# Later DMA issues, four load buffers, and the projection weights cast last, in an attention and FP4 kernel

## The reference, cut to what matters

```
xn = layernorm(x)
s  = attn(xn):      # 16 heads of 64
     q, k, v = rmsnorm(xn) @ qkv_w.T ;  q, k = exp(-0.5 q*q), exp(-0.5 k*k)
     kv  = k.T @ v  (per head, over all 2048 rows of a sequence)
     out = (q @ kv) / (q . sum(k) + 1e-6)
     x2  = xn + gamma * (out @ proj_w.T + proj_b)
     s   = x2 + gamma * (gelu(rmsnorm(x2) @ conv1_w.T + conv1_b) @ conv2_w.T + conv2_b)
g  = silu(ffn(xn)): # every operand of its matmuls quantised in blocks of 16 to FP4 values
     h = silu(Q(xn) @ Q(w_gate).T) * (Q(xn) @ Q(w_up).T) ;  ffn = Q(h) @ Q(w_down).T
out = x + s * g
Q(x): scale = max|block of 16| / 6, values rounded to 0, 0.5, 1, 1.5, 2, 3, 4, 6 times scale
```

## Time and profile before

| | |
|---|---|
| three runs, us | 1999.74, 2073.59, 1997.06 (median 1999.74) |
| profiled execution, us | 1997.77 |
| its span (slowest core, core 1), us | 1996.2; the other cores 1979.4 to 1993.6 |
| mean granted TensorE clock by core | 0.977 to 0.980 |
| busy share of the span | TensorE 94%, VectorE 82%, ScalarE 39%, GpSimd 20% |

### The profile page before, as it was taken

The page is one execution under the profiler, slowest core; times in us unless marked ns, Lnnn a source line. Parts: engine busy times, 40 slices in busy tenths (PEclk is TensorE's granted clock), DMA queues, the critical chain, the costliest instruction groups (busy, mean ns, idle before and its releaser), DMA issues.

```text
span 1996.2 us, 27757 instructions; the slowest of 8 cores (1979.4 to 1996.2 us)
## 1 busy us (share of the span) xinstructions
PE 1875.5 (94%) x9142; PEld 879.4 (44%) x9142; DVE 1636.2 (82%) x2019; ACT 785.3 (39%) x991; POOL 395.5 (20%) x356
## 2 busy tenths in 40 slices
PE   6988697878999999999999999999999999999997
PEld 3434343333444444444444444444444444444443
DVE  4788878867688688797734999999999999999986
ACT  4676576664433433544521222222222222222221
POOL 3245545534423422422500000000000000000000
PEclk9999898989999999999999999999999999999998
DMA  9788778884455465465599433444334333433322
GB/s 301 199 238 233 226 210 212 229 225 127 115 159 161 109 174 161 101 189 149 127 197 191 126 103 88 95 102 103 94 86 105 103 93 86 105 99 92 88 83 66
DMA packets 367262, 287.07 MB, mean 144 GB/s; under 512 B 299024, under 2 KB 308240, under 8 KB 366096
## 3 DMA queue, kind: packets, MB, share of 16 engines
q1 hardware_dynamic: 367120, 285.29, 55.3%
HBM read 153.63 MB, written 59.24 MB: 107 GB/s over the span
## 4 chain that ended last, share of the span: by engine, by line
PE 71%; DVE 8%; issue 7%; DMA 6%; ACT 3%; POOL 3%; SPq 2%; DVEq 0%; ACTq 0%; POOLq 0%
PE PS L1081 30%; PE PS L1126 15%; PE PS L900 10%; PE PS L883 8%; PE PS L840 5%; DMA xf<-w_gate 2%; DMA wst<-c1T 2%; PE PS L646 1%; DVE q_am L222 1%; DVE atz L817 1%; DVE ob L256 1%; PE PS L588 1%; DVE xf L231 1%; DMA xf<-w_up 1%; DMA phi_h<-pq 1%
## 5 line engine op out<-in xcount | busy, mean ns | idle before, releaser
L240 ACT ACTIVATE gam<-xf 128x1024 bf16<-128x1024 f32 (+1 forms) x196 | 198.1, 1011 | 505.1 <-DVE xf L231 494.5
L1081 PE MATMUL PS<-wg,xqT 128*128 128x512 bf16 (+1 forms) x1536 | 319.9, 361 | 1.7 <-DVE so L910 1.7
L1081 PE MATMUL PS<-wu,xqT 128*128 128x512 bf16 (+1 forms) x1536 | 319.9, 361 | 0.0
L222 DVE TENSOR_REDUCE q_am<-xf 128x64 f32<-128x1024 f32 (+1 forms) x196 | 227.6, 1161 | 74.5 <-DMA xf<-w_up 29.5
L250 DVE SCALAR_TENSOR_TENSOR xf<-gam,xf 128x1024 f32<-128x1024 bf16 (+1 forms) x196 | 233.9, 1193 | 30.0 <-ACT gam L240 29.7
L256 DVE SCALAR_TENSOR_TENSOR ob<-gam,q_sc 128x1024 bf16<-128x1024 bf16 (+1 forms) x196 | 243.0, 1240 | 3.3 <-DVE gam L253 2.8
L231 DVE SCALAR_TENSOR_TENSOR xf<-xf,q_rc 128x1024 f32<-128x1024 f32 (+1 forms) x196 | 238.0, 1214 | 1.9
L253 DVE SCALAR_TENSOR_TENSOR gam<-gam,xf 128x1024 bf16<-128x1024 bf16 (+1 forms) x196 | 235.6, 1202 | 2.1
L883 PE MATMUL PS<-xn2T,c1T_s 128*128 128x512 bf16 x1024 | 234.8, 384 | 2.4 <-DVE kvbd L566 2.4
L1126 PE MATMUL PS<-wdA,hqT 128*128 128x512 bf16 x1024 | 227.8, 380 | 0.4 <-DMA hqT<-ob 0.4
L900 PE MATMUL PS<-c2T_s,hdd 128*128 128x512 bf16 x1024 | 222.3, 379 | 0.0
(11 more groups left out here) (90 smaller groups left out, 1852.8 us busy)
## 6 DMA issues: line engine op xcount, KB each, us to landing
xx<-x SPq DMA_DIRECT2D x32, 512.0 KB, 4.5
xf<-x SPq DMA_DIRECT2D x32, 512.0 KB, 4.2
xr<-x SPq DMA_DIRECT2D x32, 512.0 KB, 4.6
out<-xr SPq DMA_DIRECT2D x31, 512.0 KB, 3.9
xa<-x SPq DMA_DIRECT2D x30, 512.0 KB, 6.0
stg<-qkvT SPq DMA_DIRECT2D x24, 512.0 KB, 13.2
xf<-w_gate SPq DMA_DIRECT2D x22, 512.0 KB, 6.3
xf<-w_up SPq DMA_DIRECT2D x22, 512.0 KB, 5.9
```

The costliest lines, as they stand in the source:

```text
L222: S.add("v", lambda v: v.tensor_reduce(am, blk(y), AX, op.max, apply_absolute_value=True), waits=[src_ev, opt("q_nq%d" % (k - 3))], ev="q_ ...
L240: S.add("sc", lambda s: s.activation(gam[k % 2][:, 0:W], xf[k % 3][:, 0:W], AF.Abs, scale=BIG), waits=["q_y%d" % k, opt("q_out%d" % (k - 2 ...
L1081: S.add("pe", lambda pe, wts=wts, bi=bi, j=j, b0=b0, ic=ic: pe.matmul(bank(b0 + j, GB[bi][1]), xqT[t % 3][:, ic, :], wts[bi][:, ic, :], st ...
```

## The change

- **Issues by SyncE.** The store of a quantised task, the store of q's result, the transpose of `turn` and the load of a tile of x are no longer emitted on SyncE's list where their data is made, but later: the first after the first step of the next period (`send`), the others at the start of the next group of matmuls (`held`).
- **Task buffers.** Tasks 0 to 27 use four buffers; the fourth lies in the place of `projT`. Their loads are emitted two tasks ahead instead of one. From task 28 on there are three buffers and one task ahead.
- **Weight jobs.** The order is now `2`, `1`, `2`, `1`, ... for 32 jobs and then the eight `p`. Jobs 0 to 19 use four buffers and their loads are emitted four ahead, after group 2; the others two, after group 1. The `p` casts wait for task 27 to leave the fourth task buffer.
- **Sequence change.** `zero_acc(1)` moves from the end of tile 16 to the end of tile 17.
- **Tail.** `turn(31)` moves from tile 27 into the tail, the loads of `phq`, `gb` move later there, that of `c2b` earlier. The last eight q groups have seven buffers instead of three.
- **Attention.** From tile 4 on its result lies in four banks with two blocks each, so `attn_z` makes one `den` and one `atz` instruction instead of three and three. `conv1` uses banks 4 to 7, the `y` pairs are (0, 1) and (2, 3). The second normalisation (`xn2`) is emitted later than the rest of `proj`, as `proj_xn2`.

```
+        xf4 = at("xf3", [P, D], F32, W1 + 12288)
+        wst = [... for i, o in enumerate([WK + 65600, WK + 69696, W3 + 24576, W3 + 28672])]
+        pqx = [at("pqx%d" % i, [P, 512], BF16, WK + 24576 + 1024 * i) for i in range(4)]
+        KX = 28
+        def xslot(k): return k % 4 if k < KX else k % 3
+        def xbuf(k): return xf4 if xslot(k) == 3 else xf[xslot(k)]
+        def xfree(k):
+            had = [j for j in range(max(k - 4, 0), k) if xslot(j) == xslot(k)]
+            return opt("q_nq%d" % had[-1]) if had else None
...
                 if n == 1:
+                    send()
                     mid()
...
+            def post(k):
+                unsent.append(lambda: store(k))
...
-                if i + 1 < len(tasks):
-                    load_task(tasks[i + 1])
+                while nload < len(tasks) and nload <= (i + 2 if nload < KX else i + 1):
+                    load_task(tasks[nload])
+                    nload += 1
...
-            S.add("sy", lambda s: s.dma_start_transpose(out=xn1T[:, c, :, :], in_=xn1_of(t)[:]),
+            later.append(lambda: S.add(
+                "sy", lambda s: s.dma_start_transpose(out=xn1T[:, c, :, :], in_=xn1_of(t)[:]),
...
+        for i in range(16):
+            wjobs += [("2", i, 0), ("1", i // 2, i % 2)]
+        wjobs += [("p", ic, 0) for ic in range(8)]
+        NW4 = 20
+        def wbuf(n): return n % 4 if n < NW4 else n % 2
...
+                w = ["wc%d" % (NW4 - 1), "wc%d" % (NW4 - 2)] if kind == "2" and ic >= 12 else \
+                    ["q_nq%d" % (KX - 1)] if kind == "p" else []
...
+        def held():
+            for fn in [later.pop(0) for _ in range(len(later))]:
+                fn()
...
         def q_group(s, qc):
+            held()
...
+            if n >= 56:
+                i = (n - 56) % 7
+                pb, sem = (pqx + [pq[2], pq[0], pq[1]])[i], "PX%d" % i
...
-                if gi == 1 and t > 4:
-                    while nl < min(nw + 2, len(wjobs)):
+                if gi == (2 if nl < NW4 else 1) and t > 4:
+                    while nl < min(nw + (4 if nl < NW4 else 2), len(wjobs)):
                         load_w(nl)
                         nl += 1
...
+            if t == 17:
+                zero_acc(1)
+            if t > 4:
+                kv_mm(t - 1)
             if t == 16:
-                kv_mm(t - 1)
                 evac(0)
-                zero_acc(1)
...
-        XB = [3, 4, 5, 2]
-        YB = [(0, 1), (6, 7)]
+        XB = [4, 5, 6, 7]
+        YB = [(0, 1), (2, 3)]
...
+            if s:
+                views = [(0, 4, 4, PS[:, 0:2048].rearrange("p (a x) -> p a x", a=4)[
+                    :, :, 0:260].rearrange("p a (h c) -> p a h c", c=65))]
...
-                          "atz3", "kvbd1_5", bfree[3], bfree[4]]
+                          "atz3", "x2_3", bfree[4]]
...
             kv_group(28 + n // 2, 2 + n % 2)
+            if n < 4:
+                proj_xn2(n)
+                turn_xn2(n)
...
+                if nxt and oc in (10, 12, 14):
+                    proj_xn2(4 * (s + 1) + (oc - 10) // 2)
```

More of the change, by code:

```diff
@@ L313, in xn_task, with send, store @@
                 tk["ev"] = "q_xn%d" % k
+        unsent = []
+        def send():
+            while unsent:
+                unsent.pop(0)()
         def stored(tk):
-            def post(k):
+            def store(k):
                 S.add("sy", lambda s: s.dma_start(out=tk["dst"], in_=ob[k % 2][:, 0:tk["W"]]),
@@ L512, in load_w @@
                 return
+            b = wbuf(n)
+            before = [m for m in range(n) if wbuf(m) == b]
             kind, ic, h = wjobs[n]
             src = {"p": "projT", "1": "c1T", "2": "c2T"}[kind]
-            S.add("sy", lambda s: s.dma_start(out=wst[n % 2][:],
+            S.add("sy", lambda s: s.dma_start(out=wst[b][:],
                                               in_=g[src][ic, :, D * h:D * (h + 1)]),
-                  waits=[opt("wc%d" % (n - 2))], inc="WS%d" % (n % 2), ev="wl%d" % n)
+                  waits=["wc%d" % before[-1] if before else "kvm3"], inc="WS%d" % b,
+                  ev="wl%d" % n)
         def cast_w(n):
             kind, ic, h = wjobs[n]
+            b = wbuf(n)
             if kind == "1":
-                S.add("sc", lambda s: s.activation(c1T[:, ic, D * h:D * (h + 1)], wst[n % 2][:],
+                S.add("sc", lambda s: s.activation(c1T[:, ic, D * h:D * (h + 1)], wst[b][:],
                                                    AF.Identity, scale=s2_fm[:, ic:ic + 1]),
@@ new lines, in attn_z @@
+            for h0, na, nh, v4 in views:
+                S.add("v", lambda v, h0=h0, na=na, nh=nh, v4=v4: v.tensor_scalar(
+                    den[b][:, h0:h0 + na * nh].rearrange("p (a h) -> p a h ()", a=na),
+                    v4[:, :, :, 64:65], 1e-6, None, op.add),
+                    waits=["at%d" % t, opt("zz%d" % (t - 2))], ev="den%d" % t)
+            S.add("v", lambda v: v.reciprocal(zz[b][:], den[b][:]),
+                  waits=["den%d" % t, opt("atz%d" % (t - 2))], ev="zz%d" % t)
@@ new lines, in attn_z @@
+            for h0, na, nh, v4 in views:
+                S.add("v", lambda v, h0=h0, na=na, nh=nh, v4=v4: v.tensor_tensor(
+                    atz[b][:, 64 * h0:64 * (h0 + na * nh)].rearrange(
+                        "p (a h e) -> p a h e", a=na, e=64),
+                    v4[:, :, :, 0:64],
+                    zz[b][:, h0:h0 + na * nh].rearrange("p (a h) -> p a h ()", a=na)
+                    .broadcast_to([P, na, nh, 64]), op.mult),
+                    waits=["zz%d" % t, opt("atT%d" % (t - 2))] +
+                          ["ps%d" % n for n in (56, 57, 58, 59, 63)], ev="atz%d" % t)
@@ L923, in build @@
             q_group(s, qc)
-            if n == 4:
+            if n == 1:
+                turn(31)
+                S.add("sy", lambda y: y.dma_start(
+                    out=c2b_t[:], in_=g["c2b"].rearrange("d -> () d").broadcast_to([P, D])),
+                    waits=["wc38"], inc="GC", ev="c2b_l")
+            if n == 8:
                 load_phq(0)
-            if n == 5:
+            if n == 10:
                 S.add("sy", lambda y: y.dma_start(
@@ L929, in build @@
                     waits=["xn1T31", "xn1T30"], inc="GB", ev="gb_l")
-                S.add("sy", lambda y: y.dma_start(
-                    out=c2b_t[:], in_=g["c2b"].rearrange("d -> () d").broadcast_to([P, D])),
-                    waits=["wc38"], inc="GC", ev="c2b_l")
                 S.add("gp", lambda p: p.tensor_tensor(gb[:], gb[:], gm[:], op.mult),
```

127 lines of the change are left out of this document (67 added, 60 removed).

## The result

The changed kernel took 1953.91 us (median of four, 1950.48 to 1954.67) against 1999.74 before. Compared on one chip the ratio is 0.9774, interval 0.975 to 0.9798: 45 us, or 2.3%. The forecast was 1948. Ratios and means of cores leave out executions and dies that ran a long stretch at a lower clock than the rest; where too few were left, no ratio is given.

A forecast was written before the change was run, and what follows sets the result against it. TensorE was busiest, its waits in the first 430 us mostly due to SyncE's order, with VectorE the limit after 209 us. Terms 12 + 38 - 7 + 5 + 2 = 50 us off 1997.8 gave 1948 us, range 1922 to 1985.

The forecast's parts named there:

- loads and issues: First 430 us: 59 of ScalarE's 96 us of waits go with more buffers and later issues, gaining 38 us.
- the zeroing: Sequence change: TensorE's 9.3 us wait for VectorE's copies goes, at 1.3 per idle us, gaining 12 us.
- covered: Deferred task stores: only ob's next writer waits, two tasks (14 us) later, so no cost was counted.
- projection casts last: Tiles 23 to 27: eight GpSimd casts instead of five slow VectorE, costing 7 us.
- 430 to 560 us: ScalarE's 5.2 us wait before the copies of v goes, less 2 us for tail loads: gain 5 us.
- attention: Attention over 28 tiles: one `atz` instead of three saves 0.28 us of VectorE each, gaining 2 us.
- the scaled task: ScalarE's waits for VectorE's scaled task: half, 16 of 31.9 us, go because its load comes earlier.
- Floor: 60 to 430 us: larger of VectorE's and TensorE's work sums to 308 of 370 us; at most 62 winnable.
- Half of it (1975): Rival: VectorE limits after the extra buffers end, so only the first stretch and zeroing gain; 1975 us, chance 0.27.
- GpSimd in tiles 23 to 27: Rival: extra casts delay the statistics there and take 15 of the 50 us; 1963 us, chance 0.12.
- Slower, by loads ahead of the transposes: Rival: earlier weight loads delay xn1T transposes in the DMA queue, 66 us lost; 2014 us, chance 0.06.
- All of it (1929): Rival: every wait on a load goes and only the floor is left, 69 us in all; 1929 us, chance 0.08.

The follow-up runs named there:

- u_zero: Changed kernel with zero_acc(1) put back to the end of tile 16; ratio to the kernel before 0.9777.
- p_zero: Kernel before with only zero_acc(1) moved to the end of tile 17; ratio to the kernel before 0.9982.
- u_now: Changed kernel with q's stores, transposes and loads of x issued at once again, task stores still late; ratio to the kernel before 0.973.
- u_order: Changed kernel with the old mixed order of weight jobs and three task buffers throughout; ratio to the kernel before 0.9832.
- u_kx: Changed kernel with three task buffers and one task ahead for all tasks; ratio to the kernel before 0.9808.

## Why the prediction was right or wrong

**Near in the total, wrong in the steps.** The sum was 50; the ratios give 45, the milestones 41.5. That is luck in part: up to tile 28 the forecast was 15 us too high, for the attention stage 9 too low. The step that failed most is that of loads and issues, 38 us forecast and about 17 measured; the next are the zeroing (12 forecast, 1 measured), which priced a stall of TensorE in a stretch that VectorE limits, and the store that was "covered" (0 forecast, 6.4 measured).

| step | forecast | measured |
|---|---|---|
| zeroing later | +12 | +1 undone (u_zero), +1 to +7 alone (p_zero) |
| loads and issues | +38 | task buffers 11, weight buffers 4 to 6, stores 1, issue order 0: about 17 |
| projection casts last | -7 | 0 to +2.6 |
| 430 to 560 us | +5 | +2.7 by milestone, +1 to +2 undone up to `conv1` |
| attention | +2 | +10.8: stores 6.4, `atz` 4.6 |

**Zeroing.** What failed was the 9.3 us wait that "goes", times 1.3, counted to the end. The wait went and 12.0 us with it (p_zero), but the same text had found VectorE the limit from 209 us on, in the very stretch. A TensorE stall in a stretch that VectorE limits is mostly made up; the two statements were not put side by side.

**Loads and issues.** Two parts of the step held: weights (40.3 to 10.1, forecast 8) and VectorE's own loads (56 to 6.6). "I take half, 16 of 31.9" for the scaled task failed: it rose to 39.6, and where a row shows it, at 236.93 us, VectorE's own work makes it late. q's stores (9.2 to 13.0) went up too. So of ScalarE's 96 us 23 went, not 59. The rest of the step, that the later issues free SyncE and with it the loads, failed in u_now: they give nothing, and SyncE stands as long behind q's results with them as without. The buffers did the work. "Statistics: `turn(31)` is emitted two groups later and more" was counted as a gain of 4 us of waits; in its place TensorE stands 9.0 us for tile 31's transpose. If the parts simply add, which nothing shows, and each has an error of some 3 us, 4.6 of the 30.1 us at `conv1` (30.1 less 11.3, 5.3, 1.6, 3.1, 1.1 and 3.1) belong to parts not undone: q's seven buffers and the moves in the tail.

**Floor.** By the prediction's own rule, the larger of VectorE's and TensorE's work in each stretch, the floor after is 130 + 95 + 82 = 307 us; 308 was forecast, and the stretches took 339.5. The size was right, though "gets no less work" hid that VectorE would lose 10 us more beside casts. Half of the 62 us above the floor was won. The floor should have cut the likeliest value, not only the high end.

**Projection casts.** The loss of VectorE was near: 4.0 us by u_order and u_kx, 6.5 forecast. "I charge all of it" failed, since the stage did not grow by it. What the new order gives back, around tile 25, u_order shows; by which wait is not settled. The 3.3 us for a cast had its own wait of 1.0 in it, so a cast can take 2.35 us from VectorE, and not 3.3.

**Attention.** Two failures. That the deferred store "is covered" looked at who waits for the store and not at what SyncE could do meanwhile; 142 us of standing there was in the trace of before, and the prediction read SyncE's waits in the first stage alone. And 1.3 for an idle microsecond was carried over from the first stage; in the attention stage the low clock behind five waits of 2.2 to 2.6 us cost another 1.6 each.

**The rivals.** Half of it (1975): by tile 23 19.3 us had come where it has 22.5; then, against it, 8 more up to tile 28 and 11 in the attention stage. GpSimd in tiles 23 to 27: its wait (`mrs`) fell from 14.9 to 10.8. Slower, by loads ahead of the transposes: apart from that of tile 31 TensorE waited once for a transpose, 2.7 us, 4.5 before, at a DMA share of up to 0.96. All of it (1929): the stretches stayed 32 us above the floor. Of the signs named, TensorE's idling (34, not under 30) and the stage's end (28 us sooner, not 35 to 50) were missed; that on weights was missed by a hair (10.1, not under 10); those on task loads, the 9.3 us and VectorE's share (89%) came true. One sign of being wrong came true as well: with tile 31 the waits for `xn1T` are 11.7 us, over 10. Its cause is not the one that the rival names.

## What to carry to other kernels

Before a stall is given a price, ask which engine's list is the longest in that stretch: a stall of another engine is made up there, and a full engine's work can be moved to a stage that has room, at the one place where nothing waits behind it. A queue that stands for a long time behind one result is worth a look in every stage, even where nobody seems to wait for that result. When work on two engines that block each other is moved, count what each instruction takes longer, on both, and not the length of one. Price an idle microsecond of TensorE from the groups that follow it in that same stage.

## What was not expected of the hardware

- A wait of 2.2 to 2.6 us of TensorE between otherwise full groups was mostly followed by a stretch at the lower clock: 16 matmuls in 5.30 us for 3.61, 1.7 us lost at half speed. The price of the clock was two thirds of that of the wait (7.9 us behind five waits of 11.9 in all, core 1 before, in the attention stage).
- One VectorE read across four PSUM banks (128x1024) took 1225 ns, in line with 547 ns for 384 elements out of one.
- A GpSimd cast of 128x1024 takes 2.35 us by itself. Beside VectorE's multiplications of two tiles the two take turns: the one that comes second waits, GpSimd 1.0 us (3.34 in all), VectorE up to 2.2 (3.38 for 1.21). The Trainium skill, page "SBUF — State Buffer", section "Who interferes with whom", says that a VectorE instruction with two SBUF inputs contends with a GpSimd one that reads SBUF, and calls the contention an exclusive lock. The trace agrees, in size too: VectorE's 2.2 us are nearly the cast's whole 2.35.
